# Cross attention of block one: the maximum pass writes its products in pairs into both PSUM banks, and one VectorE maximum reads the pair

## The reference, cut to what matters

```python
q = (h @ Wq + bq).reshape(Bx, Nx, H, D)
kv = (context @ Wkv + bkv).reshape(Bx, Mx, 2, H, D)
s = jnp.einsum('bqhd,bkhd->bhqk', q, k) * scale
p = jax.nn.softmax(s, axis=-1)
return jnp.einsum('bhqk,bkhd->bqhd', p, v)
```

## Time and profile before

| | us |
|---|---|
| median of 3 runs | 2245.24 (2241.81 to 2247.01) |
| the profiled execution, its own time | 2240.33 |
| its span, first to last instruction | 2238.7 |
| maximum pass, first piece to last reduction (L1129, L1249) | 454.1 to 1135.7 |
| VectorE reductions of the pieces (L1249), 672 | 428.8 busy |
| matmuls of the pieces (L1129), 672 | 254.5 busy |
| exponentials (L1197), 384 | 349.3 busy |

### The profile page before, as it was taken

The page is one execution under the profiler, slowest core; times in us unless marked ns, Lnnn a source line. Parts: engine busy times, 40 slices in busy tenths (PEclk is TensorE's granted clock), DMA queues, the critical chain, the costliest instruction groups (busy, mean ns, idle before and its releaser), DMA issues. The chain is left out here.

```text
span 2238.7 us, 57548 instructions
## 1 busy us (share of the span) xinstructions
PE 1898.1 (85%) x19877; PEld 1285.1 (57%) x19877; DVE 1539.0 (69%) x2708; ACT 1349.6 (60%) x2399; POOL 1006.1 (45%) x1183
## 2 busy tenths in 40 slices
PE   4888667689999999999987778655799999999988
PEld 3877334246666666666653445333466666666653
DVE  4899678666666666666642323597388888888884
ACT  2555233346666666676643333432699999999963
POOL 1333064054545545445400000152588888888840
PEclk7999788789999999999988899755799999999999
DMA  7777100033333333333201999000111111111100
GB/s 195 246 245 238 33 1 0 28 82 93 89 85 86 98 88 89 87 86 99 71 22 53 279 282 266 1 0 1 56 43 41 41 41 50 46 41 41 41 1 17
DMA packets 64287, 190.38 MB, mean 85 GB/s; under 512 B 19886, under 2 KB 27295, under 8 KB 64223
## 3 DMA queue, kind: packets, MB, share of 16 engines
q1 hardware_dynamic: 59614, 164.95, 26.4%
q0 software_dynamic: 4608, 24.58, 2.8%
HBM read 127.13 MB, written 25.49 MB: 68 GB/s over the span
## 5 line engine op out<-in xcount | busy, mean ns | idle before, releaser
L1249 DVE TENSOR_REDUCE c_part<-c_mxp 128x1 f32<-128x500 f32 x672 | 428.8, 677 | 211.5 <-PE c_mxp L1129 211.3
L1197 ACT ACTIVATE c_e<-c_stp 125x896 f32<-125x896 f32 x384 | 349.3, 917 | 167.6 <-PE c_stp L1143 166.2
L1891 ACT ACTIVATE c_e<-c_sp,alpha 128x750 f32<-128x750 f32 x448 | 392.2, 893 | 17.8 <-PE c_sp L1836 17.8
L1129 PE MATMUL c_mxp<-c_kh,c_qb 128*128 128x500 f16 x672 | 254.5, 381 | 7.1 <-DVE c_part L1249 3.7
L1927 DVE TENSOR_SCALAR c_ph<-c_e,c_inv 128x1500 f16<-128x1500 f32 x224 | 248.4, 1109 | 0.1
L1913 DVE TENSOR_SCALAR c_pt<-c_tp 125x768 bf16<-125x768 f16 x448 | 244.7, 549 | 4.0 <-issue 2.2
L1849 PE MATMUL c_tp<-ident_h,c_ph 128*128 128x128 f16 x2688 | 224.2, 220 | 17.1 <-DVE c_pt L1913 15.5
L1849 PEld LDWEIGHTS c_tp<-ident_h,c_ph 128*128 128x128 f16 x2688 | 178.0, 98 | 102.6 <-DVE c_pt L1913 57.2
L1836 PE MATMUL c_sp<-c_ki,c_qb 128*128 128x375 bf16 x896 | 218.8, 326 | 12.8 <-ACT c_e L1891 11.5
L1143 PE MATMUL c_stp<-c_qs,c_ks 103*128 103x224 f16 x1536 | 210.2, 259 | 2.5 <-ACT c_e L1197 2.5
L1143 PEld LDWEIGHTS c_stp<-c_qs,c_ks 103*128 103x128 f16 x1536 | 147.2, 98 | 71.9 <-issue 20.3
(11 more groups left out here) (276 smaller groups left out, 3624.7 us busy)
## 6 DMA issues: line engine op xcount, KB each, us to landing
c_ct<-ctx_turned SPq DMA_DIRECT2D x64, 750.0 KB
ctx_turned<-l_ct POOLq DMA_DIRECT2D x32, 750.0 KB, 4.1
c_ks<-c_kh SPq DMA_DIRECT2D x256, 93.8 KB
f_ct<-ctx_turned SPq DMA_DIRECT2D x32, 750.0 KB
l_cn<-in_ctx SPq DMA_DIRECT2D x32, 672.0 KB
f_cn<-in_ctx SPq DMA_DIRECT2D x32, 672.0 KB
c_ks<-c_kl SPq DMA_DIRECT2D x128, 93.8 KB
l_cn<-in_ctx SPq DMA_DIRECT2D x32, 78.0 KB
```

What stands on the lines that cost most here:

```text
L1129: pe.matmul(mxp[:, (PIECES * p + s) % 2, 0:500], qh[p][:, 128 * (s // 3):128 * (s // 3) + 128], kh[p][:, 500 * (s % 3):500 * (s % 3) + 500 ...
L1197: act.activation(e[:, j % (2 * GROUP), :].rearrange("p (a c) -> p a c", a=2), stp[0:KP, 2 * (j % 2):2 * (j % 2) + 2, 0:448], ACT.Exp, scal ...
L1249: dve.reduce_max(part[:, s // 3, s % 3:s % 3 + 1], mxp[:, (PIECES * p + s) % 2, 0:500], axis=AX.X).then_inc(piece_max, 1)
L1891: act.activation(e[t % E_BUFFERS][:, HALF * h:HALF * h + HALF] .rearrange("p (k c) -> p k c", k=2), sp_[:, 2 * h:2 * h + 2, 0:375], ACT.Ex ...
```

## The change

The 21 pieces of a sequence become 11 steps. Nine of them are pairs of tiles t and t + 4 (t from 0 to 2) with the same chunk of keys, the tenth is tile 3 with chunks 0 and 1, and the last is tile 3 with chunk 2 alone. TensorE writes both matmuls of a step one after the other, each into its own bank, and only the second signals; VectorE takes one maximum over 2 x 500 numbers per row and writes two. TensorE's wait for VectorE is now for the step just before. In the slot the pair stands whole ahead of the score block, and the transpose of slot 11 stands behind it.

```diff
-        PIECES = 3 * NT
+        PAIRED = [((t, k), (t + 4, k)) for t in range(3) for k in range(3)] + [((3, 0), (3, 1)), ((3, 2),)]
+        PIECES = len(PAIRED)
...
-                def piece(a, p, s, first):
+                def pieces(a, p, s, first):
                     if s == 0:
                         pe.wait_ge(k_high, 3 * a + 3)
                         pe.wait_ge(qh_spread, a + 1)
-                    if s >= 2 or not first:
-                        pe.wait_ge(piece_max, PIECES * a + s - 1)
-                    pe.matmul(mxp[:, (PIECES * p + s) % 2, 0:500], qh[p][:, 128 * (s // 3):128 * (s // 3) + 128],
-                              kh[p][:, 500 * (s % 3):500 * (s % 3) + 500], start=True, stop=True
-                              ).then_inc(piece_done, 1)
+                    if s or not first:
+                        pe.wait_ge(piece_max, PIECES * a + s)
+                    for i, (t, k) in enumerate(PAIRED[s]):
+                        c = 500 * k
+                        last = pe.matmul(mxp[:, i, 0:500], qh[p][:, 128 * t:128 * t + 128], kh[p][:, c:c + 500],
+                                         start=True, stop=True)
+                    last.then_inc(piece_done, 1)
...
+                        if live(1) and s < PIECES:
+                            pieces(n - 1, 1 - p, s, not live(2))
+                        if s >= SCORE_AT and live(2):
+                            score(n - 2, p, s - SCORE_AT, not live(3))
+                        if s < SCORE_AT and live(3):
+                            score(n - 3, 1 - p, NJ + s - SCORE_AT, False)
                         if live(1) and s == NJ - 1:
                             pe.wait_ge(top_ready, n)
                             pe.wait_ge(v_laid, 3 * n)
                             pe.transpose(pp[0:NT, 0:128], top[:, :], m.ident[:, :]).then_inc(top_turned, 1)
-                        if live(1) and 2 * s < PIECES:
-                            piece(n - 1, 1 - p, 2 * s, not live(2))
-                        if s >= SCORE_AT and live(2):
-                            score(n - 2, p, s - SCORE_AT, not live(3))
-                        if s < SCORE_AT and live(3):
-                            score(n - 3, 1 - p, NJ + s - SCORE_AT, False)
-                        if live(1) and 2 * s + 1 < PIECES:
-                            piece(n - 1, 1 - p, 2 * s + 1, not live(2))
...
-                    dve.reduce_max(part[:, s // 3, s % 3:s % 3 + 1], mxp[:, (PIECES * p + s) % 2, 0:500], axis=AX.X
-                                   ).then_inc(piece_max, 1)
+                    t, k = PAIRED[s][0]
+                    if t < 3:
+                        dve.reduce_max(part[:, t:t + 5:4, k:k + 1], mxp[:, 0:2, 0:500], axis=AX.X).then_inc(piece_max, 1)
+                    else:
+                        width = len(PAIRED[s])
+                        dve.reduce_max(part[:, t, k:k + width], mxp[:, 0:width, 0:500], axis=AX.X
+                                       ).then_inc(piece_max, 1)
```

More of the change, by code:

```diff
@@ L1243, in gather, with piece_maxima @@
                                    ).then_inc(o_out, 1)
-                def piece(a, p, s, first):
+                def piece_maxima(a, s, first):
                     dve.wait_ge(piece_done, PIECES * a + s + 1)
@@ L1260, in step @@
                             dve.tensor_copy(topt[:, :], pp[0:NT, 0:128]).then_inc(top_copied, 1)
[L1261 to L1265, removed]
+                        if live(1) and j < PIECES:
+                            piece_maxima(n - 1, j, not live(2))
+                        if live(1) and j == PIECES - 1:
                             dve.wait_ge(piece_max, PIECES * n)
```

## The result

| | us |
|---|---|
| before, median of 4 runs beside it | 2245.97 (2241.81 to 2247.01) |
| after, median of 4 runs | 2266.38 (2261.92 to 2273.6) |
| ratio after / before | 1.0099, 95% interval 1.0071 to 1.0127 |
| forecast | 2259, range 2244 to 2277 |

A second set of six runs gave 2262.76 us and a ratio of 1.0074 (1.0047 to 1.0101). Between the two profiled executions the span grew by 24.2 us, from 2238.7 to 2262.9.

A forecast was written before the change was run, and what follows sets the result against it. TensorE, 97% busy inside the stage, was taken as the bound. Full steps +7.3 us, branch +2 and edges +5 made +14.3, taken as +14 on 2245.24: 2259 us, range 2244 to 2277.

The forecast's parts named there:

- The double maximum: VectorE's one reduction over 2 x 500 numbers: 1.19 us, bounds 1.08 to 1.35, against 1.28 for two back to back.
- The link: From pair to pair, through release, matmuls and double maximum: 1.88 us, setting six slots with a projection in each step.
- Rival A: Hand-over dearer: fixed part paid twice, link 2.04 us, about 2289 us; cheaper form, as two back to back, 2275; chance 0.13.
- rivals B: Faster: the link at 1.77 us or less, six slots at TensorE's own 1.67 us, about 2219 us; chance 0.11.
- C: No difference: link between 1.78 and 1.82 us, gain and loss cancelling to within 4.5 us; chance 0.13.
- The end of the step: From last single piece to next step's first pair: 1.48 us, made of 1.37 to the transpose and 0.11 for it.
- The branch: Loop branch costs 0.30 us before the change; less covered afterwards, 0.15 us more in 14 passes, +2 us.
- The first two steps: First step with a maximum pass +2.5 us, from links and a later load; the next step +0.6 us.
- The last step: Last step with a maximum pass, without key projections: from 19.53 to about 21.5 us, +2.0 us, set by the link.
- the signs named: Double maxima 1.19 us, pairs 1.88 or 2.2 us apart, 0.38 us idle before transpose, steps 21.5, VectorE 13.3 us a step.
- Rival D: Another wait: three score blocks within 1.9 us, two exponentials between; 0.2 us short costs 6 us, about 2265; chance 0.08.
- the expected gain: Removed waste on TensorE: 0.38 us of idling before the transpose and 0.67 us of projection waits a step.

## Why the prediction was right, step by step

*The double maximum*: 1.19 us forecast from the slope of two rows, 1.20 measured. *The link*: 1.88 forecast, 1.89 to 1.90 measured, in the six slots named; the slots with value products 2.20 against 2.21. That the link costs the time, and not the order of the work, is shown from three sides: halving what the reduction reads, or splitting it, takes 23 to 28 us away, and stretching the link by one score block makes it 2.28 us as computed. Rival A (a second fixed part, or what two maxima cost back to back) is refuted by the 1.20 us, rivals B and C (a link of at most 1.77 us, or of 1.78 to 1.82) by the starts 1.89 us apart. The Trainium skill's page "Perfetto Trace Analysis" says in the section "Optimizing Scalar/DVE Operations" that breaking instructions up can let work finish sooner where an unsaturated VectorE holds up another engine; these runs agree, with 2239 us for the split maxima and 2263 to 2266 us for the merged ones. The sentence of the page "VectorE: DVE Perf Modes" of the Trainium skill, section on the errata, that the prediction cites speaks of the latency of SBUF; these maxima read PSUM, and that their fixed part is paid once is shown by this case's own 1201 ns against 677.

*The end of the step* is the term that was mis-sized. The prediction had 1.48 us from the last piece to the next pair, with 0.11 us for the transpose; it is 1.64 us in a plain step and 2.04 us with the branch, where 1.93 was forecast. I had read the 0.11 us in front of a score block, which waits for one semaphore, and put it in front of a pair that opens a new sequence and has three waits of its own; they are worked off only after the transpose is released. Their number alone does not make the cost: ahead of the loop the same three waits stand behind the first two transposes, and the pair starts 0.12 us after each. Inside the loop, where the values waited for depend on the loop's counter, it is 0.28 us, and taking the waits away from there brought the 0.11 us back. In 29 steps this is some 4 us (14 times 0.17, 13 times 0.12) of the 6.1 us by which the full steps exceed the forecast (15.4 us measured, 9.3 forecast with the branch). The rest is the hundredth of a microsecond or so by which each of the six links is longer than forecast, and the step from 0.29 to 0.25 us: the sum of the parts gave 0.29 us a step, and rounding of the starts is no reason to take less.

*The branch*: 0.4 us more than a plain step after, 0.3 before; forecast 0.45. *The first two steps*: 4.3 us against 3.1. *The last step*: 3.8 us against 2.0. By links it should have been 21.8 us; the other 1.5 us are the lower clock, which the prediction did not have: one link, from the pair at 1142.62 to the one at 1146.35, takes 3.73 us instead of 2.20. In the two kernels of this study that keep the merged maxima and change only the end of the step this step took 21.84 and 22.01 us, at a granted clock of 1.00 throughout, though TensorE idles 0.91 us before the same two pairs; with the merged maxima in the old order it took 25.94 us, 1.3 us more than a plain step, and the clock fell (0.89 and 0.68 in two windows of 4 us). So the drop hangs on more than the links or that idling; what decides it is open.

*The total*: the sum was 14.3 us, and the profiles differ by 24.2 us, the medians by 20.4. The direction and the mechanism came out as forecast, but the sum was too small by 30 to 40%, and nearly every term of it erred to the same side. The range held 2266 us because it reached up to rival A's cheaper form, and not because these terms had been allowed for. Of the signs named, steps of 21.5 us and 13.3 us of VectorE work a step were short too: they are 21.80 and 13.83 us.

*Rival D* (another wait moves in) did not come true in the changed kernel, but its mechanism, three score blocks too close for their exponentials, is what bounded the version with the piece inside the value products.

*What became of the expected gain*: the waste that the order removes was real. With the merged maximum it was filled by the new wait; with split maxima it showed as 0.16 us of a plain step, the rest being held back by the end of the step and by ScalarE.

## What to carry to other kernels

Before merging two small operations of an engine that has time to spare, add up the loop that the merged one sits in (release, producer, landing, operation) and compare it with what the bounding engine has to do in that time; here 1.89 us against 1.67 decided it. A part of an operation that hands its buffer back early can be worth more than the fixed cost that merging saves, here 0.06 us a pair. And look at how the waits stand behind an instruction that itself waits: what is queued there is worked off only after the release, and inside a loop that showed: 0.28 us instead of 0.11.

## What the runs showed of the hardware

A VectorE maximum over two PSUM banks pays its fixed part once: 1201 ns for 2 x 500 numbers and 680 ns for 2 x 250, against 677 ns for 1 x 500. In the last step TensorE's granted clock fell to 0.56 over 3.7 us (a mixture of its two levels, 1.2 and 2.4 GHz) after 0.91 us of idling before each of two pairs, and was back at 1.00 afterwards; in the kernel before, the same step ran at 1.00 throughout, and in two of the other kernels with merged maxima it did so too, with the same idling. Semaphore waits that are already satisfied are not always free where nothing covers them: behind a transpose that itself waited, three of them made the next pair start 0.28 us after it instead of 0.11 inside the loop, but 0.12 us after it where the step is written out. Whether the waits themselves or the computing of their values from the loop's counter take the time, no run separates.
